# Values multiplied six heads behind the scores, eight buffers for p, the u and z steps in other slots, and the head loop written out

## The chip, the cores and the metric

The kernel runs on one core of a Trainium2 chip (trn2). The metric is device time in microseconds (us), the median of repeated runs: 246.66 us for the kernel before, from 3 runs (246.32 to 248.56). Lower is better. The core's engines are PE (TensorE), ACT (ScalarE), DVE (VectorE), POOL (GpSimd) and SP, which here only issues transfers.

## The reference

Cross attention on 16 sequences, 8 heads, 64 channels, 256 positions, with a normalisation of x over each whole sequence and a residual:

```
mu  = mean(x, (1, 2));  var = var(x, (1, 2))
xn  = (x - mu) * rsqrt(var + 1e-5) * gamma + beta
q   = Wq xn + bq            # 8 heads x 64 channels, 256 queries
k, v = split(Wkv ctx + bkv) # 8 heads x 64 channels, 256 keys
att = softmax(q^T k / sqrt(64))
y   = att v
out = x + Wo y + bo
```

## The kernel before

The weights are folded. For each head, `t` is the normalised sequence multiplied by the product of the query and key weights (A), and `u` is the context multiplied by the product of the value and output weights (B). Scores are then context times `t`, and the sum over the heads of softmax times `u` is already the output. Everything is held as a high and a low part, so most products take two or three matmuls.

The program is a list of slots (n, h): sequence n from -3 to 17, head h from 0 to 7. All five engines walk through the same slots, each with its own code for a slot (`step`). An engine takes its instructions strictly in the order written; semaphores tie the engines together. `at(n, h, shift)` gives the head that lies `shift` heads ahead of the slot, or behind it when the shift is negative. In a slot the engines do:

- PE. In even slots the value matmuls of two heads, 24 matmuls into `ps_z` (L361 to L363; the pair that ends AV_BEHIND = 3 heads behind the slot), then `t` of two heads, 4 matmuls into `ps_t` (L383, L384; 14 heads ahead). In every slot the scores of the head, 4 matmuls into `ps_sc` (L401, L402), and the matmuls from which the row maxima are taken, 2 into `ps_max` (L420; 12 heads ahead). Once per sequence, all through the one PSUM bank `ps_m`: the transposed output `y` of sequence n-2 in slot 1 (L432), the first half of `u` of sequence n+1 in slot 3 and its second half in slot 7 (L454, L455), and the transposed maxima of sequence n+1 in slot 5 (L464).
- ACT. In even slots the copy of `t` into `t_a` (L519); in every slot two exponentials of the same scores, `p_hi` in fp16 (L527) and `p_full` in fp32 (L529). Behind the slot's exponentials: the copy of `u` into `u_hi` in slots 3 and 7 (L538), and of the transposed maxima into `neg_max_rows` in slot 5 (L545), which frees `ps_m` and raises `act_mt`.
- POOL. In every slot `p_lo` = `p_full` - `p_hi` (L609); then the first z sum `z_4` in slot 3 (L617) and the last one, `z_1`, in slot 6 (L623). In slot (1, 6) there is one `x_res` instruction on all sequences (L603). For every other one of the last 11 heads, `p_lo` is on DVE (L783).
- DVE. `t_b` (L722), the maxima `neg_max` (L738), `inv_sum` and `z_n` from `ps_z` (L733, L745), the middle sum `z_2` in slot 5 (L756), the output row of `y` in slot 1 (L768), `u_lo` in slots 3 and 7 (L776), and early on the low parts of x (L648).
- SP. Transfers of the rows of the maxima into `t_b`, of x and context of later sequences, and of results.

The waits that matter here: the value matmuls of a pair wait for `p_lo` of its second head; the scores of a head wait until `p_full` of the head two before is done (two banks of `ps_sc`); `p_full` waits for the `p_lo` two heads before (two buffers); `p_hi` waits for the value matmuls of the head four before (four buffers); a use of `ps_m` waits for the reader of the one before.

The slots of sequences 2 to 11 are a hardware loop of five turns with two sequences each (`Fori`, L217); the others are written out.

## Time and profile before

| | us |
|---|---|
| median of 3 runs | 246.66 |
| the profiled execution | 246.8 |
| its span | 245.0 |
| PE busy | 214.4 |
| DVE busy | 214.4 |
| POOL busy | 195.6 |
| ACT busy | 194.2 |

The span is the time between the first and the last recorded instruction; 1.8 us of the execution lie around it. Busy time is the sum of an engine's instructions, and for PE the ends of matmuls are modelled, so overlapping matmuls hide short gaps: the starts of successive matmuls tell more than the busy share. A wait row says which engine and line stood idle and for whom. The granted clock of TensorE is 0.99 of full speed on the mean of the span.

### The profile page before, as it was taken

To read this page: it belongs to the slowest core of one execution; us is meant where nothing else is said; L and a number is where in the kernel's file an instruction comes from. 1 tells how busy PE (TensorE), PEld (TensorE's weight loads), DVE (VectorE), ACT (ScalarE), POOL (GpSimd) and SP (SyncE) were. 2 spreads that over 40 slices of the span, in tenths; PEclk is the share of its full clock that TensorE was granted. 3 is DMA by queue.
4 is the path that set the end of the run, shared out by engine and by line. 5 is a ranking of instruction groups with operands and counts; after the bars stand their busy time and mean duration, and the time that the engine had idled before them with its cause. 6 is when DMAs were issued, how large, how long until landed. Compare 5 with 4: busy or idle time off the path is not lost.

```text
span 245.0 us, 8138 instructions
## 1 busy us (share of the span) xinstructions
PE 214.4 (87%) x2746; PEld 199.0 (81%) x2746; DVE 214.4 (87%) x447; ACT 194.2 (79%) x391; POOL 195.6 (80%) x188
## 2 busy tenths in 40 slices
PE   0663597799889999999999999999999999998962
PEld 0563476699779999999999999999999999996851
DVE  3288998999997999999999999999999999997684
ACT  2244324999788999999999999999999999999860
POOL 3036995877998998989898989898989999998580
PEclk9999999999999999999999999999999999999996
DMA  6999601121032121212121212121212121010000
GB/s 141 219 284 211 141 3 55 32 58 36 2 89 64 36 68 35 64 33 64 33 64 33 64 33 64 33 64 33 64 33 64 37 64 36 13 33 17 13 0 23
DMA packets 13412, 15.08 MB, mean 62 GB/s; under 512 B 2064, under 2 KB 11920, under 8 KB 13200
## 3 DMA queue, kind: packets, MB, share of 16 engines
q1 hardware_dynamic: 13072, 14.16, 21.9%
q10 hardware_dynamic: 320, 0.66, 1.2%
q8 instruction: 11, 0.18, 0.3%
q14 instruction: 9, 0.07, 0.1%
HBM read 5.90 MB, written 1.05 MB: 28 GB/s over the span
## 4 chain that ended last, share of the span: by engine, by line
PE 64%; DVE 11%; POOL 9%; issue 5%; DMA 4%; ACT 4%; SPq 1%; POOLq 0%
PE ps_max L420 10%; PE ps_sc L401 10%; PE ps_sc L402 10%; POOL p_lo L609 8%; PE ps_t L383 6%; PE ps_z L361 6%; PE ps_z L363 5%; PE ps_z L362 5%; PE ps_t L384 5%; DMA x_res<-x_tiles 4%; PE ps_m L455 3%; PE ps_m L454 3%; DVE neg_max L738 1%; DVE x_seq L648 1%; ACT p_full L529 1%
## 5 line engine op out<-in xcount | busy, mean ns | idle before, releaser
L609 POOL TENSOR_TENSOR p_lo<-p_full,p_hi 128x512 f16<-128x512 f32 x122 | 142.8, 1189 | 23.1 <-ACT p_full L529 23.0
L738 DVE TENSOR_REDUCE neg_max<-ps_max 128x2 f32<-128x512 f32 x128 | 84.4, 663 | 0.0
L529 ACT ACTIVATE p_full<-ps_sc 128x512 f32<-128x512 f32 x128 | 78.4, 613 | 0.5 <-POOL p_lo L609 0.5
L527 ACT ACTIVATE p_hi<-ps_sc 128x512 f16<-128x512 f32 x128 | 77.0, 602 | 1.9 <-PE ps_sc L402 1.8
L401 PE MATMUL ps_sc<-t_a,c_seq 128*128 128x256 f32 x256 | 67.8, 286 | 0.2 <-ACT p_full L529 0.2
L402 PE MATMUL ps_sc<-t_b,c_seq 65*128 65x256 f32 x256 | 67.4, 284 | 0.0
L361 PEld LDWEIGHTS ps_z<-u_hi,p_hi 128*128 128x128 f16 x512 | 46.4, 97 | 13.2 <-issue 10.8
L361 PE MATMUL ps_z<-u_hi,p_hi 128*128 128x65 f16 x512 | 52.9, 194 | 3.2 <-DVE p_lo L783 2.4
L362 PE MATMUL ps_z<-u_lo,p_hi 128*128 128x64 f16 x512 | 52.7, 192 | 0.0
L363 PE MATMUL ps_z<-u_hi,p_lo 128*128 128x65 f16 x512 | 52.7, 193 | 0.0
L519 ACT ACTIVATE t_a<-ps_t 128x512 fp32r<-128x512 f32 x60 | 35.9, 598 | 18.5 <-PE ps_t L384 17.5
L401 PEld LDWEIGHTS ps_sc<-t_a,c_seq 128*128 128x128 f32 x256 | 48.5, 189 | 0.4 <-ACT p_full L529 0.4
L402 PEld LDWEIGHTS ps_sc<-t_b,c_seq 65*128 65x128 f32 x256 | 48.6, 190 | 0.0
L722 DVE TENSOR_TENSOR t_b<-ps_t,t_a 64x512 fp32r<-64x512 f32 x60 | 40.9, 682 | 7.7 <-ACT t_a L519 5.8
L362 PEld LDWEIGHTS ps_z<-u_lo,p_hi 128*128 128x128 f16 x512 | 46.5, 98 | 0.3
L363 PEld LDWEIGHTS ps_z<-u_hi,p_lo 128*128 128x128 f16 x512 | 46.6, 97 | 0.0
L420 PE MATMUL ps_max<-c_max,t_a 128*128 128x256 f32 x224 | 45.1, 282 | 0.0
L383 PE MATMUL ps_t<-x_seq,a_hi 128*128 128x256 f32 x120 | 36.9, 329 | 6.0 <-ACT x_seq L497 3.9
L420 PEld LDWEIGHTS ps_max<-c_max,t_a 128*128 128x128 f32 x224 | 35.1, 191 | 0.0
L384 PE MATMUL ps_t<-x_seq,a_lo 128*128 128x256 f32 x120 | 31.7, 286 | 0.0
L383 PEld LDWEIGHTS ps_t<-x_seq,a_hi 128*128 128x128 f32 x120 | 23.5, 196 | 7.3 <-ACT x_seq L497 3.9
L776 DVE TENSOR_TENSOR u_lo<-ps_m,u_hi 128x512 f16<-128x512 f32 x32 | 22.0, 687 | 5.4 <-ACT u_hi L538 5.4
(101 smaller groups left out, 311.3 us busy)
## 6 DMA issues: line engine op xcount, KB each, us to landing
ctx_raw<-ctx SPq DMA_DIRECT2D x8, 256.0 KB, 17.0
c_seq<-c_all SPq DMA_DIRECT2D x16, 128.0 KB, 2.0
x_seq<-x_all SPq DMA_DIRECT2D x14, 128.0 KB, 2.0
c_max<-c_all SPq DMA_DIRECT2D x14, 128.0 KB, 2.0
x_res<-x_tiles SPq DMA_DIRECT2D x4, 256.0 KB, 7.2
z_n<-ctx_flat SPq DMA_DIRECT2D x1, 1024.0 KB, 14.7
c_seq<-c_all SPq DMA_DIRECT2D x16, 64.0 KB, 2.0
out<-x_res SPq DMA_DIRECT2D x16, 64.0 KB, 1.7
```

Of the source, the lines that this page charges most:

```text
L361: mm(ps_z[:, bank, z0:z0 + Z_W], p_hi[:, buf, kt, qs], u_h, start=(kt == 0), stop=False)
L362: mm(ps_z[:, bank, z0:z0 + C], p_hi[:, buf, kt, qs], u_l, start=False, stop=False)
L363: last = mm(ps_z[:, bank, z0:z0 + Z_W], p_lo[:, buf, kt, qs], u_h, start=False, stop=(kt == KT - 1))
L383: mm(bank[:, k * S:(k + 1) * S], a_hi[:, head + k, :], x_seq[:, q, 0, :], start=True, stop=False)
L384: last = mm(bank[:, k * S:(k + 1) * S], a_lo[:, head + k, :], x_seq[:, q, 1, :], start=False, stop=True)
L401: mm(ps_sc[:, bank, kt * S:(kt + 1) * S], c_seq[:, par, 0, keys], t_a[:, par, head, :], start=True, stop=False)
L402: last = mm(ps_sc[:, bank, kt * S:(kt + 1) * S], c_seq[0:C + 1, par, 1, keys], t_b[0:C + 1, par, head, :], start=False, stop=True)
L420: last = mm(ps_max[:, bank, qt * S:(qt + 1) * S], t_a[:, q, head, qt * P:(qt + 1) * P], c_m, start=True, stop=True)
L527: nc.scalar.activation(p_hi[:, buf, :, :].rearrange("p t s -> p (t s)"), scores, ACT.Exp).then_inc(act_phi, 1)
L529: nc.scalar.activation(p_full[:, head % 2, :], scores, ACT.Exp).then_inc(act_p, 1)
L609: nc.gpsimd.tensor_tensor(p_lo[:, buf, :, :].rearrange("p t s -> p (t s)"), p_full[:, head % 2, :], p_hi[:, buf, :, :].rearrange("p t s -> ...
L738: nc.vector.tensor_reduce(neg_max[:, (par + dn) % 2, head, :], ps_max[:, head % 2, :].rearrange("p (t s) -> p t s", t=KT), X, ALU.max, neg ...
```

## The change

Five things are changed together.

- `AV_BEHIND` goes from 3 to 5. The value matmuls of a pair and the reciprocal and `z_n` behind them move two slots later on PE and DVE.
- `p_hi` and `p_lo` have eight buffers instead of four, and the waits for the value matmuls of four heads before become waits for those of eight heads before.
- The uses of `ps_m` move: `y` from slot 1 to slot 2, the transposed maxima from slot 5 to slot 4, the first half of `u` from slot 3 to slot 5; the second half stays in slot 7. Their waits are written anew: the first half of `u` now waits for `act_mt`, that is, for ACT's copy of the maxima transposed in the slot before.
- The z sums move: `z_4` on POOL from slot 3 to 5, `z_2` on DVE from 5 to 7, `z_1` on POOL from slot 6 to slot 0 of the next sequence (two slots later).
- The loop is gone: all slots are written out. In slots of n = 1 SP no longer waits for all pieces of x and context, only for those that it moves.

```diff
-T_AHEAD, MAX_AHEAD, AV_BEHIND = 14, 12, 3
+T_AHEAD, MAX_AHEAD, AV_BEHIND = 14, 12, 5
+P_BUFS = 8
...
-        p_hi = sb("p_hi", [P, 4, KT, S], fp16)
+        p_hi = sb("p_hi", [P, P_BUFS, KT, S], fp16)
...
-            return N // CHUNK if n == FIRST - 1 else m // CHUNK + 1
+            return m // CHUNK + 1
...
-            for n in range(-3, FIRST):
+            for n in range(-3, N + 2):
                 for h in range(H):
                     step(n, n // 2, n % 2, h)
-            with eng.Fori(FIRST // 2, (LAST + 1) // 2) as pair:
...
-            if h in (3, 7) and not (isinstance(n, int) and n < 0) and (e := at(n, 0, H)):
-                return e[0], 1, h // 4
+            if h in (5, 7) and n >= 0 and (e := at(n, 0, H)):
+                return e[0], 1, h // 7
...
-                        buf = head % 4
+                        buf = head % P_BUFS
...
-                if h == 1 and (e := at(n, 0, -2 * H)):
+                if h == 2 and (e := at(n, 0, -2 * H)):
...
-                    elif kt == 0:
-                        need(pe, dma_cseq[q], 32 * fills(half, par, dn))
-                        if isinstance(n, int) and n < 2:
-                            need(pe, dve_ulo, 2 * m)
-                        else:
-                            need(pe, dve_y, n - 1)
+                    if kt == 0:
+                        pe.wait_ge(dma_cseq[q], 32 * fills(half, par, dn))
+                        pe.wait_ge(act_mt, m + 1)
...
                     else:
-                        need(pe, act_mt, n + 2)
+                        pe.wait_ge(dve_ulo, 2 * m + 1)
...
-                if h == 5 and (e := at(n, 0, H)):
-                    m, dn, _ = e
-                    need(pe, dve_max, (m + 1) * H)
-                    if isinstance(m, int) and m == 0:
-                        need(pe, dve_uscale, 1)
+                if h == 4 and (e := at(n, 0, H)):
+                    m, dn, _ = e
+                    pe.wait_ge(dve_max, (m + 1) * H)
+                    if m == 0:
+                        pe.wait_ge(dve_uscale, 1)
+                    elif m < 3:
+                        pe.wait_ge(dve_ulo, 2 * m)
                     else:
-                        need(pe, dve_ulo, 2 * m + 1)
+                        pe.wait_ge(dve_y, m - 2)
...
-                    need(act, pe_av, m * H + head - 3)
+                    need(act, pe_av, m * H + head + 1 - P_BUFS)
...
-                if h == 5 and (e := at(n, 0, H)):
+                if h == 4 and (e := at(n, 0, H)):
...
-                if h == 3 and (e := at(n, 0, -H)) and not last_sequence(e[0]):
+                if h == 5 and (e := at(n, 0, -H)) and not last_sequence(e[0]):
...
-                if h == 6 and (e := at(n, 0, -H)) and not last_sequence(e[0]):
+                if h == 0 and (e := at(n, 0, -2 * H)) and not last_sequence(e[0]):
```

What this does to the order of PE is seen around the transposed maxima. Before, in slots 4 and 5 of a sequence, the transpose (L464) stands behind both heads' scores, and value matmuls follow it; the next user of `ps_m` comes two slots later:

```order
L420 MATMUL ps_max<-c_max,t_a 128x256 [waits dve_max,act_thi,dma_cmax1]
L420 MATMUL ps_max<-c_max,t_a 128x256
L401 MATMUL ps_sc<-t_a,c_seq 128x256 [waits act_p]
L402 MATMUL ps_sc<-t_b,c_seq 128x256
L401 MATMUL ps_sc<-t_a,c_seq 128x256
L402 MATMUL ps_sc<-t_b,c_seq 128x256
L420 MATMUL ps_max<-c_max,t_a 128x256 [waits dve_max]
L420 MATMUL ps_max<-c_max,t_a 128x256
L464 MATMUL ps_m<-ident,neg_max 16x128 [waits dve_ulo,dve_max]
L361 MATMUL ps_z<-u_hi,p_hi 128x65 [waits pool_plo,dve_zn]
```

After the change, on PE in the same two slots, the transpose (now L449) is one slot earlier, and the first half of `u` (L437, L438) ends the pair:

```order
L411 MATMUL ps_max<-c_max,t_a 128x256 [waits dve_max,act_thi,dma_cmax1]
L411 MATMUL ps_max<-c_max,t_a 128x256
L449 MATMUL ps_m<-ident,neg_max 16x128 [waits dve_ulo,dve_max]
L392 MATMUL ps_sc<-t_a,c_seq 128x256 [waits act_p]
L393 MATMUL ps_sc<-t_b,c_seq 128x256
L392 MATMUL ps_sc<-t_a,c_seq 128x256
L393 MATMUL ps_sc<-t_b,c_seq 128x256
L411 MATMUL ps_max<-c_max,t_a 128x256 [waits dve_max]
L411 MATMUL ps_max<-c_max,t_a 128x256
L437 MATMUL ps_m<-b_w,c_seq 128x512 [waits act_mt,dma_cseq0]
L438 MATMUL ps_m<-b_w,c_seq 128x512
```

Between the transpose and the `u` matmuls there are now one head's four score matmuls and two `ps_max` matmuls.

On ACT, in slots 4 and 5, before: the copy of the maxima (L545) follows both heads' exponentials.

```order
L519 ACTIVATE t_a<-ps_t 128x512 [waits pe_s2,pe_t]
L527 ACTIVATE p_hi<-ps_sc 128x512 [waits pe_av,pe_s2]
L529 ACTIVATE p_full<-ps_sc 128x512 [waits pool_plo]
L527 ACTIVATE p_hi<-ps_sc 128x512 [waits pe_av,pe_s2]
L529 ACTIVATE p_full<-ps_sc 128x512 [waits pool_plo]
L545 ACTIVATE neg_max_rows<-ps_m 16x128 [waits dma_negmax1,pe_mt]
```

The same two slots on ACT after the change: the copy (L530) follows the exponentials of head 4, and `u_hi` (L523) those of head 5.

```order
L504 ACTIVATE t_a<-ps_t 128x512 [waits pe_s2,pe_t]
L512 ACTIVATE p_hi<-ps_sc 128x512 [waits pe_av,pe_s2]
L514 ACTIVATE p_full<-ps_sc 128x512 [waits pool_plo]
L530 ACTIVATE neg_max_rows<-ps_m 16x128 [waits dma_negmax0,pe_mt]
L512 ACTIVATE p_hi<-ps_sc 128x512 [waits pe_av,pe_s2]
L514 ACTIVATE p_full<-ps_sc 128x512 [waits pool_plo]
L523 ACTIVATE u_hi<-ps_m 128x8x64 [waits pool_u1,pe_av,pe_u]
```

The copy has moved up by two exponentials, and the copy of `u` has come in behind head 5.

On POOL, after the change, two `z` instructions of one sequence with the heads between them, from slot 5 of one sequence to slot 5 of the next (one row stands for several heads where it says so):

```order
L602 TENSOR_TENSOR z_4<-z_n 128x512 [waits dve_z2,dve_zn]
L594 TENSOR_TENSOR p_lo<-p_full,p_hi 128x512 [waits pe_av,act_p] x3
L608 TENSOR_TENSOR z_1<-z_2 128x128 [waits pe_y,dve_z2]
L594 TENSOR_TENSOR p_lo<-p_full,p_hi 128x512 [waits pe_av,act_p] x5
```

The three `p_lo` after `z_4` are those of heads 6, 7 and 0, so `z_1` comes right behind `p_lo` of head 0; before, it stood between those of heads 6 and 7. PE's transpose of `z_1` (L423 after the change) is in slot 2, where it was in slot 1.

## Rows read from the trace of the kernel before

**Rows 1.** Busy time of the engines in 88 to 196 us.

```profile
core 0: us, PE busy (x) PEld busy (x) DVE busy (x) ACT busy (x) POOL busy (x), PEclk, DMA share, GB/s
88.00:196.00 108.00, 108.00 (x1489) 102.33 (x1488) 101.04 (x216) 101.05 (x206) 97.71 (x91) 1.00 0.17 50
```

**Rows 2.** Chain that ended last: start us, us, what; same place in three sequences.

```profile
81.23 0.24 PE ps_max L420 x2
...
190.18 0.24 PE ps_max L420 x2
...
214.31 0.24 PE ps_max L420 x2
```

**Rows 3.** Order of time, PE, slots 4 and 5: start us, us, engine, line.

```profile
126.16 0.28 PE L401 MATMUL ps_sc<-t_a,c_seq 128*128 128x256 f32 x1
...
126.64 0.40 PE L420 MATMUL ps_max<-c_max,t_a 128*128 128x256 f32 x2
126.88 0.28 PE L401 MATMUL ps_sc<-t_a,c_seq 128*128 128x256 f32 x1
...
127.37 0.40 PE L420 MATMUL ps_max<-c_max,t_a 128*128 128x256 f32 x2
127.61 0.27 PE L464 MATMUL ps_m<-ident,neg_max 128*16 128x128 f32 x1
127.72 0.19 PE L361 MATMUL ps_z<-u_hi,p_hi 128*128 128x65 f16 x1
```

**Rows 4.** Order of time, ACT, the same two slots.

```profile
127.33 0.60 ACT L529 ACTIVATE p_full<-ps_sc 128x512 f32<-128x512 f32 x1
127.81 0.62 ACT L527 ACTIVATE p_hi<-ps_sc 128x512 f16<-128x512 f32 x1
128.28 0.63 ACT L529 ACTIVATE p_full<-ps_sc 128x512 f32<-128x512 f32 x1
128.76 0.25 ACT L545 ACTIVATE neg_max_rows<-ps_m 16x128 fp32r<-16x128 f32 x1
```

**Rows 5.** Order of time, PE, scores that had to wait for ACT.

```profile
232.88 0.39 PE L401 MATMUL ps_sc<-t_a,c_seq 128*128 128x256 f32 x1 [0.17 <-ACT p_full L529]
233.10 0.28 PE L402 MATMUL ps_sc<-t_b,c_seq 65*128 65x256 f32 x1
```

**Rows 6.** Order of time, POOL, one sequence; slot 0 begins at 132.27.

```profile
127.15 1.28 POOL L617 TENSOR_TENSOR z<-z_n 128x512 f32<-128x512 f32 x1
128.38 3.62 POOL L609 TENSOR_TENSOR p_lo<-p_full,p_hi 128x512 f16<-128x512 f32 x3
131.95 0.46 POOL L623 TENSOR_TENSOR z<-z 128x128 f32<-128x128 f32 x1
...
134.28 2.29 POOL L609 TENSOR_TENSOR p_lo<-p_full,p_hi 128x512 f16<-128x512 f32 x2 [0.74 <-ACT p_full L529]
```

**Rows 7.** Order of time, PE, scores of slots 0 and 2 of that sequence.

```profile
132.27 0.28 PE L401 MATMUL ps_sc<-t_a,c_seq 128*128 128x256 f32 x1
...
135.11 0.28 PE L401 MATMUL ps_sc<-t_a,c_seq 128*128 128x256 f32 x1
```

**Rows 8.** Waits from 88 to 196 us: engine line, awaited, us in total, times, longest.

```profile
PEld ps_z L361 <- POOL p_lo L609: 1.1, 4, 0.3
```

**Rows 9.** Waits from 52 to 76 us, and POOL in order of time there.

```profile
PE ps_t L383 <- DVE t_b L722: 0.8, 2, 0.7
PEld ps_z L361 <- POOL p_lo L609: 0.9, 1, 0.9
...
68.20 2.36 POOL L603 TENSOR_SCALAR x_res<-x_res,bo 128x2048 f32<-128x2048 f32 x1
```

**Rows 10.** Busy time of ACT alone in 217 to 237.5 us.

```profile
217.00:237.50 20.50, 18.24 (x36) 1.00 0.04 11
```

**Rows 11.** Waits from 217 us to the end.

```profile
PE ps_z L361 <- DVE p_lo L783: 2.4, 4, 1.2
```

**Rows 12.** Order of time, POOL, the last two sequences.

```profile
233.04 1.72 POOL L617 TENSOR_TENSOR z<-z_n 128x512 f32<-128x512 f32 x1
234.73 1.16 POOL L609 TENSOR_TENSOR p_lo<-p_full,p_hi 128x512 f16<-128x512 f32 x1
236.59 1.20 POOL L609 TENSOR_TENSOR p_lo<-p_full,p_hi 128x512 f16<-128x512 f32 x1 [0.71 <-ACT p_full L529]
237.74 0.90 POOL L623 TENSOR_TENSOR z<-z 128x128 f32<-128x128 f32 x1
```

**Rows 13.** The loop's line by engine: duration ns min/median/max, first and last start.

```profile
L217 PEldq COMPARE_BRANCH  x5: 83/220/251, 93.1 to 190.0; - x5
```

More of the change, by code:

```diff
@@ L87, in xattn_program @@
         wk_sb = p_full[0:C, 1, :].rearrange("p (h c) -> p h c", h=H)
-        p_hi = sb("p_hi", [P, 4, KT, S], fp16)
-        wq_bq = p_hi[0:C].rearrange("p b t s -> p (b t s)").bitcast(fp32).rearrange("p (h c) -> p h c", h=H)
-        p_lo = sb("p_lo", [P, 4, KT, S], fp16)
+        p_hi = sb("p_hi", [P, P_BUFS, KT, S], fp16)
+        wq_bq = p_hi[0:C, 0:4].rearrange("p b t s -> p (b t s)").bitcast(fp32).rearrange("p (h c) -> p h c", h=H)
+        p_lo = sb("p_lo", [P, P_BUFS, KT, S], fp16)
         inv_sum = sb("inv_sum", [P, 2, 4], fp32)
@@ L178, in chunks_by @@
         def chunks_by(n, m):
-            return N // CHUNK if n == FIRST - 1 else m // CHUNK + 1
+            return m // CHUNK + 1
         def pieces_by(n, m):
-            return len(PIECES) if n == FIRST - 1 else next(p for p, (_, end) in enumerate(PIECES) if m < end) + 1
+            return next(p for p, (_, end) in enumerate(PIECES) if m < end) + 1
         def last_sequence(m):
@@ L208, in xattn_program, with run @@
         X_LOW_AT = {(-1, 2): 2, (-1, 7): 3, (0, 1): 4, (0, 3): 5, (0, 5): 6, (1, 1): 7, (1, 3): 8}
-        FIRST, LAST = 2, 11
-        def run(eng, step):
-            for n in range(-3, FIRST):
-                for h in range(H):
-                    step(n, n // 2, n % 2, h)
-            with eng.Fori(FIRST // 2, (LAST + 1) // 2) as pair:
-                for par in range(2):
-                    for h in range(H):
-                        step(pair * 2 + par, pair, par, h)
-            for n in range(LAST + 1, N + 2):
+        def run(step):
+            for n in range(-3, N + 2):
                 for h in range(H):
@@ L548, in step @@
                     x_high(p)
[L550 removed]
+            run(step)
         @block.gpsimd
@@ L746, in step @@
                                             sums[:, :, :, 0:C], inv.broadcast_to([P, KT, 2, C]), ALU.mult).then_inc(dve_zn, 1)
-                if h == 5 and (e := at(n, 0, -H)):
+                if h == 7 and (e := at(n, 0, -H)):
                     m, dn, _ = e
@@ L760, in step @@
                         nc.vector.tensor_tensor(z_1[:], z_2[:, :, 0:C], z_2[:, :, C:2 * C], ALU.add).then_inc(dve_z1, 1)
-                if h == 1 and (e := at(n, 0, -2 * H)):
+                if h == 2 and (e := at(n, 0, -2 * H)):
                     m, dn, _ = e
```

32 lines of the change are left out of this document (13 added, 19 removed).

## The prediction

> **What bounds the kernel now.** I read the busy time by stretch first. From 88 to 196 us PE is busy for all of the 108 us, while DVE and ACT have 7 us to spare and POOL 10 [rows 1]. Busy PE time is modelled, so I looked at the pitch next. The same pair of `ps_max` matmuls starts at 81.23 and, nine sequences later, at 190.18: 12.11 us per sequence [rows 2]. The starts of PE's matmuls inside a sequence follow each other without a hole: scores of one head 0.48 us (126.16 to 126.64), its maxima 0.24, the next head 0.49 and 0.24, the transpose 0.11 [rows 3]. So between about 76 and 217 us the kernel is a full PE queue, and nothing that makes another engine freer can help there. Two stretches are different. Before 76 us PE still waits for DVE and POOL, which are late from the setup [rows 9]; after 217 us there is no `t` and little maxima work, and PE waits for `p_lo` [rows 11].
>
> The reader should see that waits which the change takes away lie at the two ends, and that any wait it adds falls, once per sequence, on the engine that has no slack.
>
> **The wait at the first half of u.** Let T be the start of the scores in slot 4. The new order on PE is scores, maxima, transpose, scores, maxima, `u`: 0.72 + 0.11 + 0.73 makes PE reach `u` at T + 1.56 (by rows: 127.61 - 126.16 = 1.45, plus 0.11 for the transpose) [rows 3]. `u` needs ACT's copy of the maxima. ACT's place for the copy is now behind `p_full` of head 4. That one starts at 127.33 = T + 1.17 and the instruction behind it at 127.81 = T + 1.65; the copy takes 0.25 [rows 4] and ends at T + 1.90. ACT can't be earlier, since its exponentials start when the scores of slot 4 come out of PE. The wait is 0.34 us, and a PE that stood still for ACT pays something to get going: 0.22 us between two score matmuls that else stand 0.12 apart [rows 5, 3], so about 0.1. I take 0.45 us per sequence, with 0.35 and 0.55 as bounds. In PE's queue everything stands behind it: the next value matmuls, `t`, scores, and so ACT and POOL. None of it can be made good, as PE is full.
>
> The other steps of `ps_m` have more room than that: `u` to `u` two slots as before, second half of `u` to `y` three, `y` to the maxima two, with one ACT and one DVE instruction to wait for. I price them at nothing. SP's transfer of the maxima starts earlier than before, its transfers for `u` have two slots more, and the reader of SP's queue, `y` (one slot later), has nothing urgent behind it.
>
> **The wait at y.** Let T0 be the start of slot 0's scores, 132.27 [rows 7]. POOL starts `p_lo` of head 0 at 134.28 = T0 + 2.01, and the next instruction some 1.12 later (two take 2.29) [rows 6]. That next one is now `z_1`, 0.46 us [rows 6]: ready at T0 + 3.59. PE has slot 2's scores at 135.11 = T0 + 2.84 [rows 7], of which 0.11 was the transpose that now comes later, so T0 + 2.73; with 0.72 for scores and maxima it is at `y` at T0 + 3.45. The wait is 0.14 plus up to 0.1 for the restart; I take 0.2 us per sequence (bounds 0 and 0.35). POOL can't start sooner: before that `p_lo` it stands idle for ACT [rows 6].
>
> **What is given back in the full stretch.** The value matmuls now have two slots more for `p_lo`. From 88 to 196 us (9 sequences) they waited for it 4 times, 1.1 us at the weight load [rows 8], of which most is overlap: the pitch shows 0.1 us every other sequence. I take 0.05 per sequence; the upper bound is 1.1 / 9 = 0.12. The deeper p buffers by themselves give nothing: `p_hi` waited for value matmuls which PE had put ahead of the same slot's scores.
>
> The loop: two sequences written out already in the kernel before, from 190.18 to 214.31, take 24.13 us, 12.07 each, against 12.11 in the loop [rows 2], though PE's branch takes 0.22 us five times [rows 13]. The branch is in the sequencer, ahead of the queued matmuls. By the trace, writing the loop out gives 0.04 x 10 = 0.4 us at most, and I count it inside the 0.05. The Trainium skill (Runtime: NRT & Kernel Launch, section "Instruction fetch mechanics") says that a taken branch out of the window that is fetched ahead costs a fetch stall, and that kernels therefore prefer full unrolling. By it this part alone would be a gain on each of five turns; the trace shows no such stall at either end of a turn, and the sum goes by the trace.
>
> **The start (up to slot (2, 6)).** PE gets back three waits, 0.8 us for `t_b` and 0.9 for `p_lo` [rows 9], 1.7 in all. Against it: the `u` wait twice, 0.9. And `z_4` and the 2.36 us of `x_res` [rows 9] now stand next to each other on POOL, so `z_1` of sequence 0 comes late and PE is held at its first `y`; I put 0.8 on it. Sum 0, between -1.7 and +1.3.
>
> **The end (from slot (14, 0)).** Here PE waited 2.4 us for DVE's `p_lo` [rows 11], and ACT was busy 18.24 of 20.5 us [rows 10]. With value matmuls two slots later that wait goes and ACT sets the pace: at best -2.3. Against it: the `u` wait, 0.45, and the `y` wait of slot (14, 2), 0.2. In slot (15, 2) the scores start as soon as `p_full` of head 0 is done, and `y` is reached 0.5 us later, while `z_1` is ready 0.15 + 1.16 + 0.46 = 1.8 after the same instant: 1.2. Last, POOL now has to do `z_4` between the last two `p_lo` that it does and then `z_1`, before PE may go on to the last value matmuls: 1.16 + 1.72 + 1.20 + 0.90 = 4.98 us from the start of `p_lo` at 234.73, where the row before ends at 238.64, so 3.9 [rows 12]: +1.1. Together +0.65; bounds -2.3 and +1.7.
>
> **The sum.** Twelve `u` waits (n = 2 to 13) at 0.45 are 5.4, eleven `y` waits (n = 3 to 13) at 0.2 are 2.2, twelve times -0.05 is -0.6, the start 0, the end +0.6: +7.6 us. Against the profiled execution, 246.8, that is 254.4; that execution lies 0.14 above the median, so 254.3 us.
>
> **The rivals.**
> - *Only the u wait shows*, with `y` hidden (its margin of 0.14 us is small): 254.3 - 2.2 - 1.2 = 250.9, slower all the same.
> - *The ends win what I say, the u wait is at its lower bound, y costs nothing*: 0.35 x 12 - 0.6 - 2.3 + 0.5 = +1.8, that is 248.5, within 1%.
> - *Faster*: ACT's copy is out before PE gets to `u`. It decides at 0.34 us: if PE reached `u` that much later in the slot (because scores of head 5 wait for something too), nothing would be lost. Then the start gives 1.7, the end 2.3 and the full stretch 0.6: 242.1. Against it: in rows 3 the scores of slot 5 follow without a hole.
> - *Nothing changes*: the stretch from 76 to 217 us is the same matmuls at the same pitch, and both ends are held by ACT and POOL: 246 to 247. It needs both new waits to be hidden, too.
>
> **Chances.** The forecast 0.58 (its own range 251.5 to 257.5), only the u wait 0.19, the 248.5 case 0.07, nothing changes 0.05, faster 0.11. A measurement of this kernel tells some 1%, 2.5 us, from no change. Slower by over 1%: 0.58 + 0.19 = 0.77; within 1%: 0.12; faster: 0.11. All low bounds together give 246.7 + 4.2 - 1.4 - 1.7 - 2.3 = 245.5, all high ones 246.7 + 6.6 + 3.9 + 1.3 + 1.7 = 260.2; the range that leaves out 2 in 10 is 248.5 to 257.5.
>
> **What would show it.** Right: a row of PE or its weight loads at the new L437 waiting for ACT's copy (L530), about 15 times and 0.3 to 0.45 us each; one at L423 for POOL's L608; a pitch of 12.7 us instead of 12.1; no more waits at L352 for `p_lo`. Wrong: a pitch of 12.1, or a first `u` matmul that follows the maxima of slot 5 within 0.25 us. From the last pair of maxima in [rows 2] to the end of the span are now 30.7 us (245.0 - 214.31); the end is right if that becomes about 31.7, with one sequence's waits in it, and under 30 would mean that ACT's pace came through.

## The result, and the profile after

| | before | after |
|---|---|---|
| median, same chip | 246.49 (245.86 to 248.56, 4 runs) | 256.85 (256.05 to 257.24, 4 runs) |
| the profiled execution | 246.8 | 256.05 |
| its span | 245.0 | 254.3 |

The ratio after to before is 1.0401, with a 95% interval from 1.0335 to 1.0467: 10 us slower by the medians, 9.25 us between the two profiled executions. The forecast was 254.3, and its range, 248.5 to 257.5, holds the time.

The head of the page after, first the span, then busy time and share of the span of each engine:

```profile
span 254.3 us, 7408 instructions
...
PE 218.1 (86%) x2746; PEld 198.9 (78%) x2746; DVE 209.9 (83%) x447; ACT 194.5 (76%) x391; POOL 198.4 (78%) x188
```

PE does the same 2746 matmuls and is busy for 3.7 us more only, in a span that is 9.3 longer. So the time is mostly idle time and not work. The busy time of the stretch that was full before, columns as in [rows 1], after the change:

```profile
88.00:196.00 108.00, 104.94 (x1410) 97.19 (x1410) 92.65 (x205) 95.86 (x196) 94.63 (x86) 1.00 0.17 50
```

PE was busy for all 108 us; now it is for 104.9 and every other engine has at least 12 us to spare. Nobody is full, and PE waits for an engine that idles a tenth of its time. That is what an order looks like in which work stands too close behind what it needs. Who is waited for is told by the waits of the whole span (engine, line, what it waited for: us in total, times, longest):

```profile
PE ps_m L437 <- ACT neg_max_rows L530: 5.2, 14, 0.8
PEld ps_m L423 <- POOL z L608: 5.2, 4, 2.1
PE ps_m L423 <- POOL z L608: 4.4, 4, 2.0
```

The first half of `u` waits for ACT's copy once per sequence, `y` for POOL's `z_1` in a few of them for long. The waits for `p_lo` in the value matmuls are gone: no row of the waits after answers to [rows 11].

**The u wait, seen in the order of time.** PE in slots 4 and 5 of one sequence (start, duration, engine, line, operation; in brackets the idle time of the engine ahead and who ended it):

```profile
140.35 0.28 PE L392 MATMUL ps_sc<-t_a,c_seq 128*128 128x256 f32 x1
...
140.82 0.40 PE L411 MATMUL ps_max<-c_max,t_a 128*128 128x256 f32 x2
141.06 0.27 PE L449 MATMUL ps_m<-ident,neg_max 128*16 128x128 f32 x1
141.09 0.36 PE L392 MATMUL ps_sc<-t_a,c_seq 128*128 128x256 f32 x1
...
141.65 0.40 PE L411 MATMUL ps_max<-c_max,t_a 128*128 128x256 f32 x2
142.39 0.47 PE L437 MATMUL ps_m<-b_w,c_seq 128*128 128x512 f32 x1 [0.34 <-ACT neg_max_rows L530]
142.70 0.40 PE L438 MATMUL ps_m<-b_w,c_seq 128*128 128x512 f32 x1
```

and ACT at the same time:

```profile
141.52 0.60 ACT L514 ACTIVATE p_full<-ps_sc 128x512 f32<-128x512 f32 x1
142.00 0.25 ACT L530 ACTIVATE neg_max_rows<-ps_m 16x128 fp32r<-16x128 f32 x1
142.15 0.57 ACT L512 ACTIVATE p_hi<-ps_sc 128x512 f16<-128x512 f32 x1
```

The maxima of slot 5 start at 141.65 and take 0.24, so `u` could start at 141.89 = T + 1.54, with T = 140.35. ACT's copy stands behind `p_full`, starts at T + 1.65 and ends at T + 1.90. `u` starts at T + 2.04: 0.50 us late. Its second half follows after 0.31, where a `u` that had not waited takes 0.23 to the next one. So a sequence pays 0.57 to 0.58 for it.

**The y wait.** PE, `y` at the end of slot 2:

```profile
137.88 0.40 PE L411 MATMUL ps_max<-c_max,t_a 128*128 128x256 f32 x2
138.16 0.33 PE L423 MATMUL ps_m<-ident,z 128*128 128x128 f32 x1
138.25 0.36 PE L392 MATMUL ps_sc<-t_a,c_seq 128*128 128x256 f32 x1
```

POOL at the same time:

```profile
136.53 1.17 POOL L594 TENSOR_TENSOR p_lo<-p_full,p_hi 128x512 f16<-128x512 f32 x1 [0.58 <-ACT p_full L514]
137.65 0.46 POOL L608 TENSOR_TENSOR z<-z 128x128 f32<-128x128 f32 x1
```

`y` starts 0.28 behind the start of the maxima instead of 0.24, just after the end of POOL's `z_1` (138.11), and the next matmul follows at 0.09 instead of the 0.03 behind the transposed maxima at 141.06. Together 0.10 us. No wait row shows it, since PE was idle for so short a time.

**The pitch.** The same `u` matmul, eight sequences apart:

```profile
91.50 0.47 PE L437 MATMUL ps_m<-b_w,c_seq 128*128 128x512 f32 x1 [0.34 <-ACT neg_max_rows L530]
...
193.28 0.47 PE L437 MATMUL ps_m<-b_w,c_seq 128*128 128x512 f32 x1 [0.34 <-ACT neg_max_rows L530]
```

101.78 / 8 = 12.72 us per sequence, against 12.11 in [rows 2]. The starts of the scores place the whole loss:

| from, to | before | after | difference |
|---|---|---|---|
| start of the span to slot (0, 0) | 43.9 | 43.2 | -0.7 |
| (0, 0) to (2, 6) | 36.7 | 37.4 | +0.7 |
| (2, 6) to (14, 0) | 136.3 | 143.1 | +6.8 |
| (14, 0) to (15, 6) | 17.6 | 18.4 | +0.8 |
| (15, 6) to the end | 10.5 | 12.1 | +1.6 |

Nearly three quarters of it lie in the full stretch, the rest at the end. The +1.6 of the last line are 1.0 up to the start of the last 24 value matmuls (5.39 us behind slot (15, 6), before 4.38) and 0.6 from there on.

**The end.** The last rows of DVE, POOL and PE that hold up the last value matmuls. DVE:

```profile
244.98 1.36 DVE L741 TENSOR_TENSOR z<-z 128x256 f32<-128x256 f32 x1 [0.62 <-POOL z L602]
246.26 0.68 DVE L768 TENSOR_TENSOR p_lo<-p_full,p_hi 128x512 f16<-128x512 f32 x1
```

POOL:

```profile
243.22 1.73 POOL L602 TENSOR_TENSOR z<-z_n 128x512 f32<-128x512 f32 x1
244.90 1.16 POOL L594 TENSOR_TENSOR p_lo<-p_full,p_hi 128x512 f16<-128x512 f32 x1
246.42 0.83 POOL L608 TENSOR_TENSOR z<-z 128x128 f32<-128x128 f32 x1 [0.36 <-DVE z L741]
```

PE:

```profile
247.31 0.33 PE L423 MATMUL ps_m<-ident,z 128*128 128x128 f32 x1 [1.99 <-POOL z L608]
247.55 0.20 PE L352 MATMUL ps_z<-u_hi,p_hi 128*128 128x65 f16 x1
```

This is a relay between two engines: `z_4` on POOL, `z_2` on DVE, `z_1` on POOL, `y` on PE, and only behind `y` the value matmuls of heads 6 and 7, which do not need it. In the relay each engine has a `p_lo` in between, and `z_2` takes 1.36 us where it has POOL's `p_lo` beside it, and 0.42 where POOL is silent (as in the run of both edits below, at 242.26).

The 0.6 us behind the relay have another source. The last 24 value matmuls of PE ran at a lower granted clock, mostly at the level of 1.2 GHz (stretch, its length, PE busy, PEclk, DMA share, GB/s; a count of 25 takes in a neighbour). After the change:

```profile
247.55:248.75 1.20, 1.20 (x24) 0.54 0.00 0
```

and the same matmuls before it, at 2.4 GHz:

```profile
238.87:239.56 0.69, 0.69 (x25) 1.00 0.00 0
```

Ahead of them PE had stood idle for 1.99 us. In the run of both edits it stood for 1.99 us too and kept a clock of 1.00 there (0.70 us for the 24), so the long wait does not always bring the lower clock.

### The profile page after: what moved, and what is told of

The parts are those of the page before. It is cut to its first block, busy times and chain, and to the rows that moved or that the text cites. A ratio compares the mean times of both kernels' runs of the same rounds, so it can differ in the third digit from the quotient of the medians.

```text
span 254.3 us, 7408 instructions
## 1 busy us (share of the span) xinstructions
PE 218.1 (86%) x2746; PEld 198.9 (78%) x2746; DVE 209.9 (83%) x447; ACT 194.5 (76%) x391; POOL 198.4 (78%) x188
## 4 chain that ended last, share of the span: by engine, by line
POOL 46%; issue 25%; DVE 12%; PE 8%; ACT 4%; DMA 4%; POOLq 1%; SPq 0%
POOL p_lo L594 36%; POOL z L602 7%; DMA x_res<-x_tiles 4%; POOL z L608 3%; DVE neg_max L723 2%; PE ps_max L411 2%; DVE t_b L707 2%; ACT t_a L504 1%; DVE a_lo L639 1%; DVE xn L626 1%; DVE tops L683 1%; DVE x_all L633 1%; PE ps_m L437 1%; ACT p_full L514 1%; DVE var L663 1%
## 5 line engine op out<-in xcount | busy, mean ns | idle before, releaser
L594 POOL TENSOR_TENSOR p_lo<-p_full,p_hi 128x512 f16<-128x512 f32 x122 | 144.5, 1201 | 29.9 <-ACT p_full L514 29.6
L392 PE MATMUL ps_sc<-t_a,c_seq 128*128 128x256 f32 x256 | 70.2, 296 | 0.2 <-ACT p_full L514 0.2
L352 PE MATMUL ps_z<-u_hi,p_hi 128*128 128x65 f16 x512 | 53.9, 196 | 0.0
L353 PE MATMUL ps_z<-u_lo,p_hi 128*128 128x64 f16 x512 | 53.3, 193 | 0.0
L392 PEld LDWEIGHTS ps_sc<-t_a,c_seq 128*128 128x128 f32 x256 | 49.3, 192 | 1.0 <-ACT p_full L514 0.4
```

Of the source, the lines that this page charges most:

```text
L352: mm(ps_z[:, bank, z0:z0 + Z_W], p_hi[:, buf, kt, qs], u_h, start=(kt == 0), stop=False)
L353: mm(ps_z[:, bank, z0:z0 + C], p_hi[:, buf, kt, qs], u_l, start=False, stop=False)
L392: mm(ps_sc[:, bank, kt * S:(kt + 1) * S], c_seq[:, par, 0, keys], t_a[:, par, head, :], start=True, stop=False)
L594: nc.gpsimd.tensor_tensor(p_lo[:, buf, :, :].rearrange("p t s -> p (t s)"), p_full[:, head % 2, :], p_hi[:, buf, :, :].rearrange("p t s -> ...
```

## The experiments

The theory: PE is full from 76 to 217 us, and the change puts two waits into it, the `u` wait (ACT's copy stands one exponential too late) and the `y` wait (`z_1` one subtraction too late). Loop, buffers and the later value matmuls neither cost nor give much there. Rival theories: the eight buffers or the longer program cost the time; or six heads' distance does (`AV_BEHIND` = 5: the first head of a pair is six behind the slot); or the whole `u` and z plan is too tight, and mending one wait only uncovers the next. Medians of before that a kernel is compared with are 246.35 (19 runs) for the first four, 246.54 (29 runs) for the next four, and 246.89 (23 runs) for the last two. The pitch is always that from slot (4, 0) to (13, 0), over nine.

### The loop alone, written out

The kernel before with this edit alone:

```diff
-            for n in range(-3, FIRST):
-                for h in range(H):
-                    step(n, n // 2, n % 2, h)
-            with eng.Fori(FIRST // 2, (LAST + 1) // 2) as pair:
-                for par in range(2):
-                    for h in range(H):
-                        step(pair * 2 + par, pair, par, h)
-            for n in range(LAST + 1, N + 2):
+            for n in range(-3, N + 2):
```

> The kernel before with one edit: the loop is written out, all else stays (four buffers, values four heads behind, u and z in their old slots). My theory, from the two sequences that were written out already and took 12.07 us each against 12.11: between 246.0 and 246.6 us, pitch 12.05 to 12.1. Rival, by the Trainium skill (Runtime: NRT & Kernel Launch, Instruction fetch mechanics): each taken branch costs a fetch stall, so writing out gains at five turns; then under 245.5. Second rival: fetching twice the instructions slows the start, and some of the 10 us that the whole change cost comes from here: over 248.

Measured: 245.75 (244.72 to 249.18, 10 runs), ratio 0.9959 [0.9923, 0.9996]. The pitch is 12.076 against 12.101, which is 0.3 us over the span. A part of the difference lies ahead of slot (0, 0), where executions of one kernel differ as well, so no more than the 0.3 can be put down to the loop. The median lies 0.25 us under the expected range and above the 245.5 of the rival. The longer program costs nothing that can be seen, and the loop costs 0.025 us per sequence.

### ACT's copy one exponential earlier

The kernel after, with the copy of the transposed maxima between `p_hi` and `p_full` of slot 4 instead of behind both:

```diff
+            def copy_maxima(n, half, par, h):
+                if h == 4 and (e := at(n, 0, H)):
...
+                    nc.scalar.activation(neg_max_rows[:, q, :], ps_m[0:H * KT, 0:P], ACT.Copy).then_inc(act_mt, 1)
...
                     nc.scalar.activation(p_hi[:, buf, :, :].rearrange("p t s -> p (t s)"), scores, ACT.Exp).then_inc(act_phi, 1)
+                    copy_maxima(n, half, par, h)
                     lo_done(act, m, head - 2)
                     nc.scalar.activation(p_full[:, head % 2, :], scores, ACT.Exp).then_inc(act_p, 1)
...
-                if h == 4 and (e := at(n, 0, H)):
...
-                    nc.scalar.activation(neg_max_rows[:, q, :], ps_m[0:H * KT, 0:P], ACT.Copy).then_inc(act_mt, 1)
```

> The changed kernel with one instruction moved on ACT: the copy of the transposed maxima stands between p_hi and p_full of head 4 instead of behind p_full. Theory: the u wait is ACT's late copy alone. The copy is then done at T + 1.42, before PE's T + 1.56, the 0.50 us ahead of L437 goes from every sequence, and the pitch falls from 12.74 to 12.25 us; with the waits at the start and in slot (14, 5) 6.0 to 7.5 us less: 249.5 to 251 us. Rival: delaying p_full of head 4 by 0.2 us moves the loss to POOL or to the scores of slot 6, and less than half of it comes back: over 253.

Measured: 249.45 (249.05 to 250.3, 4 runs), ratio 1.0106 [1.0033, 1.0179]: 7.4 us less than after. The pitch falls from 12.72 to 12.25. ACT in slot 4, its new order:

```profile
127.81 0.25 ACT L505 ACTIVATE neg_max_rows<-ps_m 16x128 fp32r<-16x128 f32 x1
127.97 0.57 ACT L523 ACTIVATE p_full<-ps_sc 128x512 f32<-128x512 f32 x1
```

and the busy time from 88 to 196 us:

```profile
88.00:196.00 108.00, 108.00 (x1461) 101.20 (x1460) 97.05 (x213) 99.43 (x204) 96.76 (x88) 1.00 0.18 52
```

PE is full again, and no wait of `u` for the copy is left in this stretch. So the 0.47 us per sequence were this one instruction's place on ACT. That it was the place, and not that ACT had too much to do, is plain from the fact that ACT does the same work in both.

### z_1 ahead of p_lo

The kernel after, with `z_1` at the head of POOL's slot 0 instead of at its foot:

```diff
+                if h == 0 and (e := at(n, 0, -2 * H)) and not last_sequence(e[0]):
...
+                    nc.gpsimd.tensor_tensor(z_1[:], z_2[:, :, 0:C], z_2[:, :, C:2 * C], ALU.add).then_inc(pool_z1, 1)
                 if (e := at(n, h, 0)) and not (isinstance(e[0], int) and e[0] * H + e[2] in LO_ON_VECTOR):
...
-                if h == 0 and (e := at(n, 0, -2 * H)) and not last_sequence(e[0]):
...
-                    nc.gpsimd.tensor_tensor(z_1[:], z_2[:, :, 0:C], z_2[:, :, C:2 * C], ALU.add).then_inc(pool_z1, 1)
```

> The changed kernel with one instruction moved on POOL: z_1 stands ahead of p_lo of head 0 instead of behind it. Theory: POOL is idle there (0.7 us before that p_lo), so z_1 is out 1.5 us before PE wants it, and the wait ahead of L423 goes: 0.14 to 0.2 us in each of 11 sequences, 0.8 at the first y, up to 1.5 in slot (15, 2): 3 to 4 us less, 253 to 254 us, pitch 12.6. Rival: the y wait was too small to count and its time returns at the next wait: above 255.5.

Measured: 252.26 (252.08 to 252.7, 4 runs), ratio 1.0228 [1.0154, 1.0301]: 4.6 us less than after, a little more than expected. POOL in slot 0:

```profile
135.31 0.45 POOL L593 TENSOR_TENSOR z<-z 128x128 f32<-128x128 f32 x1
...
135.94 2.29 POOL L599 TENSOR_TENSOR p_lo<-p_full,p_hi 128x512 f16<-128x512 f32 x2 [0.17 <-ACT p_full L514]
```

`z_1` now fills the time in which POOL waited for ACT anyway (0.74 in [rows 6], 0.17 here), and costs `p_lo` nothing. In the full stretch this gives 0.09 per sequence, 1.0 us; 2.4 us come from slot (14, 0) to the end (28.1 against 30.5), where `y` of slot (15, 2) no longer has a `p_lo` ahead of its `z_1`, and 1.0 between slots (0, 0) and (2, 6), where the first `y` was held. (Ahead of slot (0, 0) this execution is 0.7 longer than that of after, by nothing that was edited.)

### Both

The kernel after with both edits.

> Both moves together on the changed kernel. Theory: the two waits are independent and are all that the full stretch lost, so the pitch is back at 12.05 to 12.15 us and the two gains add up: 9 to 11 us less, 246 to 248 us. What is then left against the kernel before is the end. Rival: the eight buffers and six heads of distance themselves cost something (a later z_n, other PSUM timing), so the pitch stays above 12.25 with no wait row that names a cause.

Measured: 245.97 (245.13 to 248.24, 10 runs), ratio 0.998 [0.9944, 1.0016]: 10.9 us less than after, and the same as before. Alone the two gave 7.4 and 4.6, which is 1.1 more. So two instructions in another place, one on ACT and one on POOL, undo the whole loss while everything else of the change stays. The `u` matmul, without a wait ahead of it:

```profile
91.70 0.47 PE L437 MATMUL ps_m<-b_w,c_seq 128*128 128x512 f32 x1
```

Its second half still follows late, as its duration of 0.47 shows. The pitch is 12.161 where the old order written out has 12.076: 0.085 us per sequence are left. They lie at this matmul. It starts 0.14 us behind the end of ACT's copy, which makes it 0.03 late, and its second half follows 0.08 late; the profile counts no wait. (That is 0.11; by subtraction some 0.02 are gained elsewhere.)

### The copy one exponential later

The kernel after with ACT's copy behind `p_hi` of slot 5, the edit as above with one number changed:

```diff
-                if h == 4 and (e := at(n, 0, H)):
+                if h == 5 and (e := at(n, 0, H)):
```

> The changed kernel with ACT's copy of the maxima one exponential later (behind p_hi of head 5), the opposite of e2. Theory: the wait is ACT's order and nothing else, so a further exponential, 0.48 us from start to start, adds in full: 0.98 us ahead of L437 instead of 0.50, pitch 13.2, 14 or 15 times 0.48 more: 263.5 to 264.5 us. Rival: part of the 0.50 is another wait that is there anyway (transfer of the context, has nothing to do with the copy); then the pitch rises by less than 0.4.

Measured: 263.4 (262.36 and 264.44, 2 runs), ratio 1.0668 [1.0574, 1.0763], pitch 13.21. PE:

```profile
93.48 0.47 PE L437 MATMUL ps_m<-b_w,c_seq 128*128 128x512 f32 x1 [0.82 <-ACT neg_max_rows L505]
```

ACT:

```profile
92.61 0.62 ACT L520 ACTIVATE p_hi<-ps_sc 128x512 f16<-128x512 f32 x1
93.08 0.25 ACT L505 ACTIVATE neg_max_rows<-ps_m 16x128 fp32r<-16x128 f32 x1
```

The three places of the copy, each one exponential (0.48 us from start to start) behind the other, give pitches of 12.25, 12.72 and 13.21. Every step costs what ACT's instruction takes. This is the proof that the wait passes into the time undiminished.

### The buffers alone

The old order written out, with eight buffers for `p_hi` and `p_lo`, the value matmuls where they were:

```diff
-        p_hi = sb("p_hi", [P, 4, KT, S], fp16)
+        p_hi = sb("p_hi", [P, 8, KT, S], fp16)
...
-                    need(act, pe_av, m * H + head - 3)
+                    need(act, pe_av, m * H + head - 7)
```

(and likewise for `p_lo` and in the places that read them)

> The kernel of e1 (kernel before, loop written out) with eight p buffers instead of four, values still four heads behind, nothing else. Theory: p_hi never waited for a free buffer, so nothing: the same as e1 within 0.5 us, 245.2 to 246.3. Rival: the waits for pe_av did hold ACT at the end, where its rows show idle time; then 1 us or more less.

Measured: 246.56 (245.0 to 248.82, 10 runs), ratio 0.9995 [0.9949, 1.0042]. The pitch is 12.075, against 12.076 without them: in the full stretch the deeper buffers alone neither give nor cost. The time lies 0.3 us above the expected range. In the profiled execution the end, from slot (14, 0) on, is 28.9 us against 28.0 of the written-out kernel, and 0.6 of these 0.9 are the last 24 value matmuls, which took 1.28 us at a granted clock of 0.50 (1.2 GHz) instead of 0.69 at 1.00. That is no doing of the buffers as far as any row shows.

### The value matmuls back at their old distance

The kernel with both edits, and only the distance undone:

```diff
-T_AHEAD, MAX_AHEAD, AV_BEHIND = 14, 12, 5
+T_AHEAD, MAX_AHEAD, AV_BEHIND = 14, 12, 3
```

> The kernel of e4 (changed kernel with both moves) with one number back: values three heads behind the scores instead of five. It tells what the distance is worth by itself. Theory: nothing in the full stretch beyond the small waits for p_lo (pitch at most 0.1 us above e4's 12.17), and at the end PE waits for p_lo again, so the scores of slot (15, 6) come 1.0 to 1.6 us later than in e4; with the value matmuls two slots earlier one of the z sums' waits shrinks at the very end. 246.5 to 247.5 us. Rival: the distance costs something at the start, where value matmuls no longer fill the wait for t_b; then this kernel is at or under e4, 245.0 to 246.0.

Measured: 249.2 (247.61 to 252.47, 10 runs), ratio 1.0101 [1.0056, 1.0146]: 3.2 us more than with six heads' distance, much more than expected. The pitch hardly moves (12.20 against 12.16). The profiled execution, which is 3.3 us above the median of its kernel, has its loss at both ends: from (0, 0) to (2, 6) 38.7 us against 36.1, from (14, 0) to the end 29.2 against 27.7, 4.5 with the full stretch. Two parts of that go with a lower granted clock: 0.60 from 76 to 80 us, where the loss grows from 1.9 at slot (2, 2) to 2.6 at slot (2, 6), and 0.50 at the last 24 value matmuls, which took 1.22 us instead of 0.70. They are 1.2 us together, about what the 4.5 exceed the 3.2 of the medians by; whether other executions had them is not shown. At the start the value matmuls wait for `z_n` of the heads before. PE:

```profile
75.03 0.19 PE L352 MATMUL ps_z<-u_hi,p_hi 128*128 128x65 f16 x1 [1.80 <-DVE z_n L733]
```

DVE:

```profile
71.53 1.23 DVE L744 TENSOR_TENSOR z<-z 128x256 f32<-128x256 f32 x1
...
74.55 0.40 DVE L733 TENSOR_TENSOR z_n<-ps_z,inv_sum 128x256 f32<-128x256 f32 x1
```

POOL:

```profile
70.51 1.98 POOL L592 TENSOR_SCALAR x_res<-x_res,bo 128x2048 f32<-128x2048 f32 x1
```

`z_2` took 1.23 us, until POOL's long `x_res` was through, and all of DVE behind it came later. With six heads' distance DVE does the very same there:

```profile
71.61 1.24 DVE L744 TENSOR_TENSOR z<-z 128x256 f32<-128x256 f32 x1
```

and that `z_n` starts as late, at 74.64; but PE does not stand for it, since its value matmuls come two slots later, while here it stood for 1.80. So the distance is what hides this late `z_n`. It is no loss and, with the new z plan, worth about 3 us by the medians, little of it in the full stretch. The theory had the part at the end (1.0 to 1.6 us up to slot (15, 6), in the trace 1.7) and none at the start.

### The end, reordered

The kernel with both edits; for sequence 14, the last but one, DVE's `z_2` now stands behind DVE's last `p_lo`, and `y` (PE) and its output row (DVE, by the same edit) stand two slots later:

```diff
-                if h == 2 and (e := at(n, 0, -2 * H)):
+                if h == (4 if n == N else 2) and (e := at(n, 0, -2 * H)):
...
-                if h == 7 and (e := at(n, 0, -H)):
+                if h == 7 and n != N - 1 and (e := at(n, 0, -H)):
...
+                if (n, h) == (N - 1, 7):
+                    need(dve, pool_z4, n)
+                    nc.vector.tensor_tensor(z_2[:], z_4[:, :, 0:2 * C], z_4[:, :, 2 * C:4 * C], ALU.add).then_inc(dve_z2, 1)
```

> The kernel of e4 with the end alone put in another order: z_2 of sequence 14 on DVE behind p_lo of the last head instead of ahead of it, and y of sequence 14 on PE and its result row on DVE behind the last value matmuls instead of ahead. Theory: the last value matmuls then wait for the last p_lo alone and start 0.15 us after it, not behind z_2 (1.36 us) and z_1 (0.83): 0.9 to 1.3 us less than e4, and this is the version that beats both kernels, 244.7 to 245.2 us. Rival: the end is held by the chain of sums behind it, and y of sequence 14 takes the saved time from the last z sums: less than 0.4 us.

Measured: 246.04 (245.15 to 248.52, 12 runs), ratio 0.9975 [0.994, 1.001]. The expected gain is not there: 27.9 us from (14, 0) to the end, against 27.7. PE no longer waits for `y`, but in its place for `z_n`:

```profile
237.07 0.20 PE L352 MATMUL ps_z<-u_hi,p_hi 128*128 128x65 f16 x1 [2.23 <-DVE z_n L733]
```

DVE, what stands ahead of that `z_n`:

```profile
234.55 1.57 DVE L771 TENSOR_TENSOR p_lo<-p_full,p_hi 128x512 f16<-128x512 f32 x1 [0.67 <-ACT p_full L523]
236.04 0.41 DVE L775 TENSOR_TENSOR z<-z 128x256 f32<-128x256 f32 x1
...
236.58 0.42 DVE L733 TENSOR_TENSOR z_n<-ps_z,inv_sum 128x256 f32<-128x256 f32 x1
```

POOL:

```profile
234.42 1.15 POOL L603 TENSOR_TENSOR p_lo<-p_full,p_hi 128x512 f16<-128x512 f32 x1
```

DVE's `p_lo` takes 0.68 us in the row of after above. Here it starts 0.13 behind POOL's, and takes 1.57. The reordering put both engines' `p_lo` side by side, and `z_n` behind them.

### The last p_lo behind the z_n that PE waits for

The kernel above, with DVE's last `p_lo` and `z_2` moved from slot (15, 7) to (16, 0), behind the `z_n` of that slot:

```diff
-                if isinstance(n, int) and n * H + h in LO_ON_VECTOR:
...
+                lo = n * H + h
                 if (n, h) == (N - 1, 7):
-                    need(dve, pool_z4, n)
+                    lo = -1
+                if (n, h) == (N, 0):
+                    lo = N * H - 1
+                if lo in LO_ON_VECTOR:
...
+                if (n, h) == (N, 0):
+                    need(dve, pool_z4, N - 1)
```

> The kernel of e6 with one more change of order at the end: on DVE the inv_sum and z_n of heads 2 and 3 of the last sequence stand ahead of the last head's p_lo, and z_2 of sequence 14 behind it, all in slot (16, 0). Theory, from e6's rows: the last value matmuls start at 237.07 because they wait for that z_n (the bank of ps_z), which stood in DVE's queue behind a p_lo of 1.57 us and z_2; the p_lo itself was done 0.9 us sooner. In the new order they start 0.15 us behind p_lo: 0.7 to 0.9 us less than e6, 245.1 to 245.4 us. Rival: the time goes to z_1 and y of sequence 14 or to a slower p_lo, and nothing changes.

Measured: 245.21 (244.02 to 246.41, 12 runs), ratio 0.9948 [0.9918, 0.9978], so it is faster than before by half a per cent. From (15, 6) to the end it needs 10.83 us against 11.63 above, as expected, both with a clock of 1.00 at the last value matmuls; the intervals of the two ratios overlap, so it is this stretch and not the medians that tells the two kernels apart. PE:

```profile
237.05 0.19 PE L352 MATMUL ps_z<-u_hi,p_hi 128*128 128x65 f16 x1 [1.44 <-DVE p_lo L777]
```

DVE:

```profile
235.09 0.42 DVE L733 TENSOR_TENSOR z_n<-ps_z,inv_sum 128x256 f32<-128x256 f32 x1
235.43 1.47 DVE L777 TENSOR_TENSOR p_lo<-p_full,p_hi 128x512 f16<-128x512 f32 x1
```

PE now waits for `p_lo` itself, which again has POOL's beside it.

### y behind an odd head

The kernel above, with `y` and its output row in slot 3 instead of 2, so that value matmuls and not scores follow it:

```diff
-                if h == (4 if n == N else 2) and (e := at(n, 0, -2 * H)):
+                if h == (4 if n == N else 3) and (e := at(n, 0, -2 * H)):
```

> The kernel of e9 with y (PE) and its result row (DVE) in slot 3 instead of slot 2. In e4 the first score matmul behind a transpose is followed by the next after 0.20 us instead of 0.12, while value matmuls behind a transpose (as in the kernel before) start at their usual distance. Theory: y now stands ahead of value matmuls again, so 0.08 us come back per sequence: pitch 12.16 to 12.08, 1.0 us less than e9, 244.2 to 244.5 us, and this is the fastest version. Rival: y one slot nearer to the transposed maxima makes that transpose wait for DVE's result row, and the pitch stays or rises.

Measured: 245.24 (244.11 to 246.06, 12 runs), ratio 0.9919 [0.9879, 0.9959], pitch 12.152 against 12.170. The expected 0.08 per sequence did not come. A transpose costs the same 0.11 us on either side: ahead of value matmuls it is 0.11 to the next start, and these follow each other in 0.03 as ever; ahead of scores it is 0.03, and then 0.20 instead of 0.12 for the first of them. As to speed the two last kernels can't be told apart. Both are faster than the kernel before and the kernel after the change, but not clearly faster than the old order with its loop written out (0.9959, with an interval that overlaps theirs).

## Why the prediction was right, step by step

- **The bound.** A full PE queue from 76 to 217 us, in which an added wait falls on the time undiminished: shown by the three places of the copy (12.25, 12.72, 13.21 for steps of 0.48).
- **The u wait**, put at 0.45 with 0.35 to 0.55: it is 0.50 at the start and 0.07 to 0.08 at the next matmul, 0.57 or a little more. ACT's copy starts at T + 1.65 and ends at T + 1.90, exactly as forecast, and PE is ready at T + 1.54, so the 0.34 worked out was 0.36. (The 0.34 in the brackets of the row is counted from a modelled end, 142.05, and agrees by chance.) The term was low because getting going again costs 0.2 and not the 0.1 from [rows 5]: PE starts 0.14 after the copy's end, and its second half comes 0.07 late. Moving the copy won back 0.47 of it; the other 0.085 is still there when the copy comes in just in time.
- **The y wait**, put at 0.2: it is 0.10 (12.25 to 12.16 when `z_1` is moved on top of the copy, and 12.72 to 12.63 without). The scores of slot 0 start at T0 = 134.67 (135.16, where the maxima of that slot start, less 0.48), so PE is at `y` at 138.12 = T0 + 3.45, as worked out. POOL's `p_lo` was early: T0 + 1.86 instead of T0 + 2.01. It follows ACT's `p_full`, in both kernels after a wait of POOL, and that ends at T0 + 1.78 instead of T0 + 1.84; the other 0.09 are not explained by any row. So `z_1` was ready at T0 + 3.44 and the wait was all restart. The two errors, 0.12 too low for `u` and 0.10 too high for `y`, cancel, which is luck: 0.57 + 0.10 - 0.05 = 0.62, the measured 12.72 - 12.10, where the forecast had 0.60.
- **What is given back**, 0.05 per sequence: 0.025 of it is the loop, measured by itself. That the rest comes from the later value matmuls is likely and not proven: with `AV_BEHIND` back at 3 the pitch was 12.20 against 12.16, in an execution 3.3 us above its median, while the buffers alone gave nothing (12.075 against 12.076). It is at most a few hundredths.
- **The rival that only the u wait shows** (250.9): the `y` wait is half of what was put, but not nothing; its larger price lies at the end. With `z_1` moved the kernel ran in 252.26. The **248.5 case** is out, since the `u` wait is above its upper bound and the `y` wait not zero. **Faster** and **nothing changes** are out: PE came to `u` at T + 1.54, two hundredths earlier than the T + 1.56 worked out, and not 0.34 later.
- **The loop.** Neither a stall at the turns before nor a cost of the longer program after. The rule of the Trainium skill (Runtime: NRT & Kernel Launch, section "Instruction fetch mechanics") would have made unrolling a gain on each of five turns; the written-out kernel measured 0.9959 [0.9923, 0.9996], of which the pitch explains 0.3 us, so the trace does not show the stall that the page describes.
- **The start**, put at 0: from the start of the span to slot (2, 6) it is 80.6 us in both, but this is luck. It is a sum of -0.7 ahead of slot (0, 0), where the change moves nothing on purpose and the kernels of this case lie anywhere from 41.9 to 45.4, and of +0.7 behind it. The +0.7 can be taken apart by the runs: moving the copy alone gives back 0.9, `z_1` alone 1.0, both 1.3, and with both the stretch is 0.7 shorter than before. So the `u` waits (put at 0.9) and the first `y` (0.8) were priced well one by one, though they overlap, and the three waits that PE gets back brought 0.7 and not 1.7.
- **The end** is the term that was mis-sized: put at +0.6, it came to +2.4. Up to slot (15, 6) the forecast was -2.3 + 0.45 + 0.2 + 1.2 = -0.45 and the trace has +0.8. All three waits there are longer: 0.98 for the copy in slot (14, 5) instead of 0.45, 0.56 instead of 0.2 at `y` of slot (14, 2), and 1.57 instead of 1.2 at `y` of slot (15, 2). Taken off, they leave 2.3 for what is given back, as forecast. The `y` of slot (14, 2):

```profile
226.46 0.40 PE L411 MATMUL ps_max<-c_max,t_a 128*128 128x256 f32 x2
227.20 0.33 PE L423 MATMUL ps_m<-ident,z 128*128 128x128 f32 x1 [0.34 <-POOL z L608]
```

  It starts 0.74 behind the maxima instead of 0.24, and its restart costs 0.06 more. `z_1` ends 3.42 us behind the scores of slot 0, as in the full stretch (3.44); but slot 2 has no `t` left, so PE has the scores of slot 2 after 2.18 us instead of 2.73. It is the same at `u` of slot (14, 5): the copy ends at T + 1.98, hardly later than the T + 1.90 of the full stretch, while PE, without maxima matmuls, is there at T + 1.14 instead of T + 1.54. The failing step is that the waits of the full stretch were carried into a stretch where PE has less to do in a slot, comes earlier, and so waits longer.
- From (15, 6) on the end was put at +1.1 and is +1.6. The relay is +1.0 of it, and POOL's chain, from its `p_lo` at 242.10 to the end of `z_1`, took 5.15 us, with 0.36 of waiting for `z_2` in it, where the sum had 4.98; this part was right within the size of its terms. The other 0.6 are the last value matmuls at the lower clock and what waits for them; the sum had no such term.
- The sign of the end's term was right, and from the maxima pair of [rows 2] that started at 214.31 it is now 33.1 us to the end of the span (254.3 - 221.2) where 31.7 was forecast. With both waits mended the end was 27.7 us from slot (14, 0), where the written-out old order has 28.0, a difference too small to be read from one execution of each.
- The median, 256.85, is 2.5 us above the forecast: some 1.8 are the end, 0.8 the distance from the profiled execution to the median.

The speed lost is thus shown to be two places: ACT's copy (7.4 us alone), POOL's `z_1` (4.6 alone), 10.9 both. What remains open is the 0.085 us per sequence at `u`; a copy that comes earlier still would need the transpose itself in an earlier slot, and this wasn't tried.

## What to carry to other kernels

Where one engine's queue is full, look in a reordering for the tightest producer that it now waits for, and work that wait out from starts inside the slot: the position of a 0.25 us copy, ahead of or behind a 0.48 us instruction, was worth 3% here. Put small instructions that the full engine waits for ahead of long ones that it doesn't need yet, best where the other engine would idle anyway. Price the ends of the program apart, since there the full engine has less to do in a slot, comes earlier to what it needs, and waits longer for it than in the steady part.
